# Expert stage: 32 slots of 128 tokens and seven half slots of 64 instead of 39 slots of 128, with a ring of four for the first weights

## The reference

```python
aff = x @ centroids.T                  # x: 4096 tokens, normalized; 8 centroids
assign = argmax(aff, axis=1)           # every token goes to one expert
alpha = sigmoid(aff of that expert)
for e in range(8):
    h = layernorm(xs, ln_g[e], ln_b[e])
    h = relu(h @ w1[e].T + b1[e])      # 256 -> 1024
    ye = xs + h @ w2[e].T + b2[e]      # 1024 -> 256
out = alpha * y + (1 - alpha) * xs     # per token, y = ye of its own expert
```

## Time and profile before

| | |
|---|---|
| median of three runs | 892.99 us (892.44 to 894.5) |
| profiled execution | 890.49 us, of which the span of its instructions is 888.7 us |
| busy, share of the span | PE 94%, PE's weight loads 59%, DVE 67%, ACT 56%, POOL 37% |
| chain that ended last | PE 33% of the span, of it L1855 16% and L1875 15% |
| mean granted clock of TensorE | 0.985 |

### The profile page before, as it was taken

The page is one execution under the profiler, slowest core; times in us unless marked ns, Lnnn a source line. Parts: engine busy times, 40 slices in busy tenths (PEclk is TensorE's granted clock), DMA queues, the critical chain, the costliest instruction groups (busy, mean ns, idle before and its releaser), DMA issues. The chain is left out here.

```text
span 888.7 us, 24625 instructions
## 1 busy us (share of the span) xinstructions
PE 835.6 (94%) x8767; PEld 524.4 (59%) x8768; DVE 597.9 (67%) x1133; ACT 497.6 (56%) x1168; POOL 327.6 (37%) x469
## 2 busy tenths in 40 slices
PE   6999859999989999999999988789999999999995
PEld 4555433444434444434444434569999999999994
DVE  4888999898878898988888902966433333333331
ACT  4668426777767777777877795024333333333330
POOL 9999663343233434324243431634111111111111
PEclk9999988999999999999999999999999999999998
DMA  8578632553433333322333323968555555555540
GB/s 280 156 234 260 180 110 77 175 169 87 107 87 87 98 87 99 81 79 72 89 92 96 113 41 101 294 236 256 199 182 178 177 177 178 182 183 178 177 173 0
DMA packets 62643, 129.50 MB, mean 146 GB/s; under 512 B 16217, under 2 KB 43482, under 8 KB 56282
## 3 DMA queue, kind: packets, MB, share of 16 engines
q1 hardware_dynamic: 58282, 112.99, 42.4%
q0 software_dynamic: 4272, 15.29, 4.7%
HBM read 100.35 MB, written 23.44 MB: 139 GB/s over the span
## 5 line engine op out<-in xcount | busy, mean ns | idle before, releaser
L891 ACT ACTIVATE arena<-ps_pair 128x512 f32<-128x512 f32 (+2 forms) x640 | 308.6, 565 | 99.9 <-PE ps_pair L1214 96.7
L971 DVE TENSOR_REDUCE B_block_max<-ps_item 128x8 f32<-128x1024 f32 x288 | 338.1, 1220 | 32.4 <-PE ps_item L1118 31.4
L1214 PE MATMUL ps_pair<-q_stack,k_stack 99*32 99x512 bf16 (+7 forms) x3072 | 191.5, 333 | 9.2 <-ACT arena L891 5.5
L805 POOL TENSOR_SCALAR_AFFINE_SELECT arena<-arena 128x256 f32<-128x256 f32 x256 | 102.9, 408 | 164.5 <-ACT arena L891 160.3
L1214 PEld LDWEIGHTS ps_pair<-q_stack,k_stack 99*32 99x32 bf16 (+1 forms) x3072 | 79.0, 96 | 134.0 <-ACT arena L891 88.6
L1231 PE MATMUL ps_pair<-arena,B_v_quad 128*32 128x512 f32 (+3 forms) x1536 | 153.9, 494 | 1.2 <-ACT B_oacc L910 0.5
L1855 PEld LDWEIGHTS C_bank<-arena 128*128 128x128 f32 x1248 | 146.1, 193 | 1.9
L1855 PE MATMUL C_bank<-arena 128*128 128x128 f32 x1248 | 146.4, 276 | 0.0
L1875 PE MATMUL C_ps_p<-arena 128*128 x624 | 141.0, 379 | 0.0
L1875 PEld LDWEIGHTS C_ps_p<-arena 128*128 128x128 f32 x624 | 115.6, 190 | 14.1
L1507 ACT ACTIVATE arena<-C_bank,ffn_columns 128x128 f32<-128x128 f32 x156 | 44.5, 368 | 141.7 <-PE C_bank L1855 141.7
(11 more groups left out here) (168 smaller groups left out, 672.6 us busy)
## 6 DMA issues: line engine op xcount, KB each, us to landing
arena<-in_w_exp SPq DMA_DIRECT2D x41, 1024.0 KB, 5.0
qk_parts<-arena SPq DMA_DIRECT2D x32, 384.0 KB, 3.4
q_stack<-qk_parts SPq DMA_DIRECT2D x96, 128.0 KB, 3.0
k_stack<-qk_parts SPq DMA_DIRECT2D x64, 128.0 KB, 3.0
arena<-in_w_exp POOLq DMA_DIRECT2D x6, 1024.0 KB, 6.9
rows<-payload SPq DMA_DIRECT2D x39, 130.5 KB, 2.1
arena<-in_x SPq DMA_DIRECT2D x8, 512.0 KB, 5.1
arena<-in_x_feat SPq DMA_DIRECT2D x8, 512.0 KB, 6.1
```

Source lines behind the costliest of these rows:

```text
L805: pool.affine_select(out=block_p, in_=block_p, compare_op=ALU.is_ge, fill=0.0, base=0, pattern=[[0, 2], [1, P]], channel_multiplier=-1).th ...
L891: act.activation(pr[s % PR][:, h:h + 2 * n - 1:2, 0:W], ps_s[(EXPS * Q.const + exps_to[s] + u) % R][:, 0:n * W].rearrange("p (h n) -> p h ...
L971: dve.tensor_reduce(bmx[:, g:QH:GH, first:first + 3 * gap + 1:gap], src[:, :, :].rearrange("p c (b n) -> p c b n", n=P), AX.X, ALU.max).th ...
L1214: mm = pe.matmul(bank[at:at + 32, :], ks[rows, r, half, bass.ds(g * SEQ + kb * P + at, 32)], qs[rows, r, half, bass.ds(g * SEQ + c * QW + ...
```

## The change

Slots 0 to 31 stay as they are. The last seven become half slots of at most 64 tokens; what an expert has beyond its full slots goes to one or two of these. In a half slot:

- Hidden product: the 64 tokens are stationary and 256 columns of the first weights move; two column strips of 64 take different halves of the hidden features. 8 matmuls. The result has tokens on partitions, so ACT and DVE copy one bank each (128x256) to SBUF, PE turns it with four transposes, and ACT and DVE evict four times 128x64 each with bias and relu.
- The 64 rows are loaded as 128 partitions of 128 features (half the features of a token each), by two DMAs, so one transpose turns them.
- Output product: 64 tokens stationary, 128 columns of second weights moving, two strips for the two halves of the output features. 16 matmuls. The second weights come from a copy per half slot, made by POOL in steps 24 to 30 (2048 columns each).
- PE's order in step n is: hidden product of n, rows of n+1, output product of n-1, the four transposes of n.

First weights have a ring of four and are loaded three slots ahead; the ring's third and fourth place lie over attention results, so the load for slot 2 waits for all projections. The loop holds the steps 4 to 23; 24 to 39 are written out. The table's chain has 16 instead of 8 entries per slot.

```diff
-NSLOT = (NTOK + NE * (P - 1)) // P
+FULL, HALVES = NTOK // P, NE - 1
+HT = P // 2
+NSLOT = FULL + HALVES
...
+W1R = 4
+W1_AHEAD = 3
...
-        w1b = arena[:, NE * W2C:NE * W2C + 2 * W1C].rearrange("p (r n) -> p r n", r=2)
+        w1b = arena[:, NE * W2C:NE * W2C + W1R * W1C].rearrange("p (r n) -> p r n", r=W1R)
...
+            if is_half(S):
+                sp.dma_start(rows[:, S.ring(RD), 0:HT * 2],
+                             pay_d[bass.ds(at, HT), 0:DIM].rearrange("t (a n) -> a t n", a=DC)).then_inc(s_rl[S.ring(RD)], 16)
+                sp.dma_start(rows[:, S.ring(RD), DIM:PAYW],
+                             pay_d[bass.ds(at, HT), DIM:PAYW].unsqueeze(0).to_broadcast([DC, HT, PAYW - DIM])).then_inc(s_rl[S.ring(RD)], 16)
...
+        COPY_AT = FULL - 2 * RD
...
-            run_steps(eng, emit, -1, RD, NSLOT - 3, NSLOT + 1, RD)
+            run_steps(eng, emit, -1, RD, COPY_AT, NSLOT + 1, RD)
...
                 def emit(n):
-                    S = n + 2
+                    S, W = n + 2, n + W1_AHEAD
+                    if W.const == FIRST_SLOTS:
+                        sp.wait_ge(s_tab, 4)
...
-                    if S.within(NSLOT) and (S.reg is not None or S.const >= 2):
-
-                        wait(sp, s_m1[1], n, 1, 1, alone=gate)
-                        load_w1(sp, S)
+                    if W.within(NSLOT):
+                        if n.reg is None and n.const == -1:
+                            sp.wait_ge(s_pj, NT)
+                        else:
+                            wait(sp, s_m1[1], n, 1, 1, alone=gate)
+                        load_w1(sp, W)
...
+                    if n.reg is None and COPY_AT <= n.const < COPY_AT + HALVES:
...
+                        k = n.const - COPY_AT
+                        e = expert(pool, Step(FULL + k))
+                        pool.tensor_copy(own[k], w2s[:, bass.ds(e * W2C, W2C)]).then_inc(s_own, 1)
...
+                def copy_hidden(S):
+                    act.wait_ge(s_m1[0], S.const + 1)
+                    if S.const >= FULL + 2:
+                        act.wait_ge(s_ht[0], S.const - FULL - 1)
+                    act.activation(hid[:, S.const % 2, 0:DIM], bank[:, 0, 0:DIM], ACT.Copy).then_inc(s_hc[0], 1)
+
+                def half_relu(S):
+                    e = expert_of(act, S, known)
+                    act.wait_ge(s_ht[0], S.const - FULL + 1)
+                    act.wait_ge(s_m2, S.const - 1)
+                    for k in range(HC // 2):
+                        for j in range(2):
+                            c = HC * j + k
+                            act.activation(hr[:, S.ring(2), c, 0:HT], ps_t[0][:, k, j, :], ACT.Relu,
+                                           bias=col[:, bass.ds(e, 1), 2 * DC + c]).then_inc(s_r[0], 1)
...
                     normalize(n + 2)
                     S = n
+                    if is_half(S) and S.within(NSLOT):
+                        half_relu(S)
...
+                        if is_half(n) and n.within(NSLOT):
+                            half_relu(n)
                         wait(dve, s_m2, S, 1, 1)
                         wait(dve, s_res, S, 1, -1)
-                        dve.tensor_tensor(y[:, S.ring(2), :], ps_y[S.ring(2)], b2r[:, bass.ds(e * DIM, DIM)], ALU.add).then_inc(s_y, 1)
+                        add_bias(S, e)
...
+                def half_hidden(S):
+                    wait(pe, s_xt, S, DC, DC)
+                    wait_dma(pe, s_w1, S)
+                    for i in range(2):
...
+                        for c in range(DC):
+                            for j in range(2):
+                                at = c * FF + j * QW + i * DIM
+                                mm = pe.matmul(bank[j * HT:(j + 1) * HT, i, 0:DIM], xT[:, S.ring(2), c, 0:HT], w1b[:, S.ring(W1R), at:at + DIM],
+                                               start=(c == 0), stop=(c == DC - 1), tile_position=(0, j * HT))
+                        mm.then_inc(s_m1[i], 1)
+
+                def turn_hidden(S):
+                    i = S.const % 2
+                    for k in range(HC):
+                        if k % 2 == 0:
+                            pe.wait_ge(s_hc[k // 2], S.const - FULL + 1)
+                        mm = pe.transpose(ps_t[k // 2][:, k % 2, :, :].rearrange("p a t -> p (a t)"), hid[:, i, k * P:(k + 1) * P], ident)
+                        if k % 2 == 1:
+                            mm.then_inc(s_ht[k // 2], 1)
+
+                def half_output(S):
+                    r, w2 = S.ring(2), own[S.const - FULL]
+                    pe.wait_ge(s_own, S.const - FULL + 1)
+                    order = [HC * j + k for k in range(HC) for j in range(2)]
+                    for i, c in enumerate(order):
+                        if i % HC == 0:
+                            wait(pe, s_r[i // HC], S, HC, HC)
+                        for a in range(DC):
+                            mm = pe.matmul(ps_y[r][a * HT:(a + 1) * HT, 0:P], hr[:, r, c, 0:HT], w2[:, c * DIM + a * P:c * DIM + (a + 1) * P],
+                                           start=(i == 0), stop=(i == FC - 1), tile_position=(0, a * HT))
+                    mm.then_inc(s_m2, 1)
```

More of the change, by code:

```diff
@@ L1291, in phase_route_experts @@
         cnt = sb("cnt", [1, 2, NE])
-        more = sb("more", [1, NE, NT])
+        more = sb("more", [1, 2, NE, NT])
         ns = sb("ns", [1, 4, NE])
-        step = sb("step", [1, 3, NE])
+        step = sb("step", [1, 2, NE])
         used = sb("used", [1, NE + 1])
         tail0 = sb("used_rows", [1, 1])
[L1297 to L1300, removed]
+        ends = sb("ends", [1, 2 * NE + 1])
+        leap = sb("leap", [1, 2, 2 * NE])
+        tri = sb("tri", [1, 2, NE, NE])
+        cum = sb("cum", [1, 2, NE])
+        over = sb("over", [1, 1])
+        entry = sb("entry", [1, REST])
+        shift = sb("shift", [1, REST])
+        tables = spare_room[0:1, W2C:W2C + 4 * REST * 2 * NE].rearrange("p (j s v) -> p j s v", j=4, s=REST)
+        tab, tab2 = tables[:, 3, :, :], tables[:, 0:3, :, :]
         es = sb("es", [1, 4, REST])
+        own = [xr[:, :, :].rearrange("p t n -> p (t n)")[:, i * W2C:(i + 1) * W2C] for i in range(4)]
+        own += [spare_room[:, i * W2C:(i + 1) * W2C] for i in range(2)]
+        own += [sb("second_weights", [P, W2C])[:, :]]
+        assert len(own) == HALVES
         HC = FC // 2
@@ L1472, in normalize @@
                         row = rows[:, S.ring(RD), :]
-                        act.activation(zz[:, S.ring(2), :], row[:, 0:DIM], ACT.Identity, bias=row[:, COL_B:COL_B + 1],
+                        n = P if is_half(S) else DIM
+                        act.activation(zz[:, S.ring(2), 0:n], row[:, 0:n], ACT.Identity, bias=row[:, COL_B:COL_B + 1],
                                        scale=row[:, COL_S:COL_S + 1]).then_inc(s_zz, 1)
@@ L1693, in rest_table @@
[L1693 to L1698 removed]
+                    dve.wait_ge(s_t2, 17)
@@ L1871, in emit @@
                         wait(pe, s_y, S, 1, -1)
-                        for c in range(FC):
-                            if c % HC == 0:
-                                wait(pe, s_r[c // HC], S, HC, HC)
-                            mm = pe.matmul(ps_y[r], hr[:, r, c, :], w2s[:, bass.ds(e * W2C + c * DIM, DIM)],
-                                           start=(c == 0), stop=(c == FC - 1))
-                        mm.then_inc(s_m2, 1)
+                        if is_half(S):
+                            half_output(S)
+                        else:
+                            for c in range(FC):
+                                if c % HC == 0:
+                                    wait(pe, s_r[c // HC], S, HC, HC)
+                                mm = pe.matmul(ps_y[r], hr[:, r, c, :], w2s[:, bass.ds(e * W2C + c * DIM, DIM)],
+                                               start=(c == 0), stop=(c == FC - 1))
+                            mm.then_inc(s_m2, 1)
+                    if is_half(n) and n.within(NSLOT):
+                        turn_hidden(n)
                 steps(pe, emit)
```

252 lines of the change are left out of this document (176 added, 76 removed).

## The result

The changed kernel takes 880.61 us (median; 877.11 to 883.26) where the kernel before takes 892.72 (four runs): a ratio of 0.9878 [0.9848, 0.9907], 95% interval, so a gain of 1.2% that is clear of the noise. Timed again later it was 879.81, ratio 0.9878 [0.9854, 0.9903]. The profiled execution took 880.16 us (span 878.4), 10.3 less than the 890.49 of before. The forecast was 877.3 and a saving of 15.7.

A forecast was written before the change was run, and what follows sets the result against it. PE was taken to bound the expert stage at 7.25 us per slot. Saving 17.9, less 1.2 for row stalls and 1.0 at the end, gave 15.7 us, so 877.3 us; range 872.5 to 886.5, about 82%.

The forecast's parts named there:

- What bounds it, and what is rewritten: Expert stage: PE bounds at 7.25 us per slot; the 54.1 us from slot 32's hidden product on are rewritten.
- A half slot on PE: Half step on PE: 1.73 hidden, 1.74 output, 0.55 transposes, 0.56 for strips, 4.58 us against 7.25.
- visit to the strips: Half-slot products: going into column strips and out again costs 0.28 us each time, twice per half slot.
- The sum without stalls: Steps 32 to 39 on PE: 36.2 us in all, 17.9 less than 54.1.
- landing takes 2.1: Half-slot row loads land 2.1 us after issue, so PE stalls 1.2 us in all for rows 35 to 38.
- Rival 3: Half steps: 1 MB loads ahead make rows land after 5.0 us, stalls 6.8 instead of 1.2, 882.9; 13% with similar stalls.
- And the relus: ACT in half steps: relus queue behind normalization's wait for rows, delaying the output product 0.5 to 0.6 us.
- The end: After PE's last product: last output DMA issued 2.9 us later instead of 1.9, 1.0 us lost.
- Edits costed at nothing: Ring of four, longer table, POOL's copies, halved rows and outputs: costed at nothing, with covers named.
- rival 4: Gain lost at the covers of uncosted edits or in unlooped code: about 890 to 893, 4%; slower, 2%.
- Rival 1: Half-slot hidden and output products: two strips run one after the other, 3.5 us more per half slot, 900.4; 5%.
- Rival 2: Half-slot products: weight loads don't hide behind products, 18.5 us more, 895.8; 4%.

The follow-up runs named there:

- e2: Changed kernel without loading the first weights of slots 35 to 38; stretch from slot 32 to the last output product 40.6 us against 42.4.
- e8: Changed kernel with rows by three 64-partition DMAs, result before relus on DVE, relus before normalization on ACT; stretch from slot 32 37.1 us against 42.4.
- e5: Changed kernel with a first-weight ring of two, loaded two slots ahead; stretch from slot 32 42.5 us, about 1.6 of it from a lower clock.

## Why the prediction was right, and where it was wrong

- *What bounds it, and what is rewritten.* Right: the first 32 slots are 7.25 us apart as before, and all of the gain lies behind slot 32.
- *A half slot on PE.* 4.58 forecast, 4.62 measured (own row buffers). The agreement is partly luck, for two of its parts were off and cancel: a product with its visit to the strips takes 1.88 and 1.90 instead of 2.01 and 2.02, so a visit costs about 0.15 us, not 0.28; the five transposes take 0.25 + 0.59 = 0.84 instead of 0.55.
- *The sum without stalls.* 36.2 forecast, 36.4 measured. Steps 32, 38 and 39 were given 6.02, 4.19 and 3.1; 6.03, 4.21 and 3.03 came.
- *Rows, the step that failed: "landing takes 2.1".* It gave 1.2 us of stalls; 6.0 were measured. The step up to it held: in step 35 (T = 842.25) slot 33's result leaves the buffer at T+2.05 where T+2.0 was given, and the second DMA is issued at T+3.6. Normalization of slot 37 then starts at T+7.6, not T+5.5:

```profile
843.95 0.35 DVE L1924 SCALAR_TENSOR_TENSOR C_res<-C_y,C_al,rows 128x128 f32<-128x128 f32 x1
```

```profile
849.81 0.49 ACT L1534 ACTIVATE arena<-rows 128x128 f32<-128x128 f32 x1 [3.77 <-DMA rows<-payload]
```

  The 2.1 is the landing of a load with 128 partitions outermost. The half-row load has another pattern and no row in the trace of before; it should have been bounded as a new operation, not priced at a full slot's and waved through as "fewer bytes".
- *Rival 3* named this wait with 6.8 us, and its size is nearly what came; the sign given for it, PE idle before the output product and ACT idle before normalization for a row DMA, is what the profile shows. Its cause holds for less than a third: without weights in front 4.2 of the 6.0 us stay (e2). So 880.6 lies inside the range, but nearer to this rival's 882.9 than to the forecast's 877.3, and the range held because its bounds took this wait in, for a reason that was mostly another.
- *And the relus.* That they queue behind the normalization was in the text, as one delay; PE saw it twice in a step, before the rows' turning and before the output product, and in the old buffers both were gone, but for 0.51 us, only when landing, result and order were all mended (e8).
- *The end.* 1.0 lost was forecast, 0.9 came.
- *Edits costed at nothing.* Held: slot 2's rows were turned at 603.53 with no idle time before, PE waited neither for the table nor for POOL's copies, and the ring of four changes nothing (e5). So nothing is seen of rival 4 either. Only the halved rows, put down as fewer bytes, did cost time, as above.
- *Rivals 1 and 2.* Rival 1 was priced at 900.4, and one strip measures 899.53; the price was right, the condition false. Rival 2's condition is false as well: weight loads hide behind products in strips, 16 records in 1.87 us.

Of the 15.7 us, 10.3 came in the profiled execution. Of the missing 5.4, 4.8 went to the rows, 0.4 to the later start of slot 32, 0.2 to the sum without stalls. In the second profile of the changed kernel the rows cost 1.0 less.

## What to carry to other kernels

Here a DMA's landing time followed its pattern more than its bytes: look at what is outermost on both sides, and price a pattern that no trace has shown yet as a new operation. When a stage's steps get shorter, go round the loop of each buffer (result, load, landing, use) with the new step; here a load that cost PE nothing at steps of 7.25 us was the bound at 4.6. And look at what stands in an engine's order behind the instruction that will wait.

## What the hardware showed

- Two fp32 strips of 64 columns run side by side: 1.88 us for what takes 3.60 on one strip.
- A load of half the bytes, with two halves outermost, kept 1.2 to 1.8 DMA engines busy and came 4.2 to 5.5 us after its first issue (3.8 to 4.4 with no weights beside it); one with 128 partitions outermost kept 10 busy and came after 2.1.
- The scatter of a half slot's output, 128 pieces of 512 bytes, is not slow by its pieces: it landed after 2.1 to 4.9 us where a full slot's took 2.4. Over the seven half slots of the changed kernel:

```profile
DMA to landing us min/median/max: 2.1/2.4/4.9
```

The first three (4.3 to 4.9) ran beside half-row and weight loads, and so did the two full slots' scatters before them (4.3 and 4.4); the last four, after the loads, took 2.1 to 2.4. Loads beside it are not all of it: in e2 one took 3.4 us with neither kind on the way. PE waited for none of them.
